# A linear-attention stage reordered: keys projected before the gate, and routing logits computed as 8 extra columns of the output product

## The reference

```
xxx = tanh((x + dx * maa_x) @ maa_w1);  mw, mk, mv, mr, mg = xxx_f @ maa_w2_f      # 5 factors
xf  = x + dx * (maa_f + m_f)                                                       # 5 inputs
r, k, v = xr @ W_r.T, xk @ W_k.T, xv @ W_v.T;  g = silu(xg @ W_g.T)
w = time_decay + tanh(xw @ decay_w1) @ decay_w2;  cs = cumsum(-exp(w))
A = lower ? (r*exp(cf)) (k*exp(-cf))^T : (r*exp(-cb)) (k*exp(cb))^T;  y = A @ v    # 16 heads of 8
y = groupnorm(y) * g @ W_o.T
x = layernorm(x + y)
logits = x @ gate_w.T;  probs = softmax(logits);  two best of 8 experts            # router of layer 2
```

## Time and profile before

| what | us |
|---|---|
| three timed runs | 1278.52, 1280.97, 1282.59 |
| median | 1280.97 |
| profiled execution, its own time | 1271.11 |
| its span | 1268.8 |
| the stage's first attention scores | 42.90 |
| the stage's last scatter instruction | ends near 392 |

### The profile page before, as it was taken

The page is one execution under the profiler, slowest core; times in us unless marked ns, Lnnn a source line. Parts: engine busy times, 40 slices in busy tenths (PEclk is TensorE's granted clock), DMA queues, the critical chain, the costliest instruction groups (busy, mean ns, idle before and its releaser), DMA issues. The chain is left out here.

```text
span 1268.8 us, 34315 instructions
## 1 busy us (share of the span) xinstructions
PE 963.4 (76%) x12701; PEld 681.3 (54%) x12702; DVE 799.1 (63%) x2290; ACT 576.5 (45%) x1143; POOL 490.6 (39%) x597
## 2 busy tenths in 40 slices
PE   6789999989852999972455463948899999614996
PEld 2456665666642999870222222737556665313885
DVE  3656777687553555542888885873587666852665
ACT  1454555555421555542555563323564443313664
POOL 0113434543472444444335330002034443443776
PEclk8787878889755999996667665975997675756998
DMA  2122212327011222213223123013211115001110
GB/s 88 34 60 68 77 37 59 85 69 221 21 45 54 62 58 57 60 33 97 43 51 74 42 34 104 26 67 98 69 55 53 52 52 176 11 15 51 54 53 23
DMA packets 121827, 78.88 MB, mean 62 GB/s; under 512 B 46947, under 2 KB 108361, under 8 KB 121312
## 3 DMA queue, kind: packets, MB, share of 16 engines
q1 hardware_dynamic: 115040, 64.36, 18.9%
q0 software_dynamic: 6656, 12.70, 3.2%
HBM read 48.46 MB, written 27.51 MB: 60 GB/s over the span
## 5 line engine op out<-in xcount | busy, mean ns | idle before, releaser
L1117 ACT ACTIVATE bx_h<-bx_up,bx_cur 128x128 f32<-128x128 f32 x288 | 82.3, 368 | 103.7 <-PE bx_up L1088 103.7
L571 POOL DMA_INDIRECT regions_b<-a_xo,a_seat x64 | 64.7, 1012 | 140.3 <-DVE a_seat L864 123.3
L686 ACT ACTIVATE a_at<-a_scores 128x1024 f32<-128x1024 f32 x64 | 65.6, 1025 | 99.6 <-PE a_scores L445 99.0
L1046 POOL DMA_INDIRECT chosen_b<-bx_ys,bx_to x72 | 75.5, 1048 | 91.1 <-DVE bx_ys L1160 91.1
L1088 PE MATMUL bx_up<-bx_xT,bx_cur 128*128 128x128 f32 x576 | 82.7, 287 | 0.7 <-DVE bx_cur L1133 0.2
L1070 PE MATMUL bx_down<-bk_w,bx_h 128*128 x576 | 82.0, 285 | 0.6 <-ACT bx_h L1117 0.4
L440 PE MATMUL a_scores<-a_rk,a_kx 32*128 32x128 f32 (+3 forms) x1024 | 64.9, 327 | 20.9 <-DVE a_kx L753 11.9
L1088 PEld LDWEIGHTS bx_up<-bx_xT,bx_cur 128*128 128x128 f32 x576 | 71.3, 195 | 10.5 <-issue 5.4
L1325 PE MATMUL c_bank<-c_sq,c_con 128*128 128x512 f32 x32 | 30.2, 1100 | 61.1 <-DVE keep_attn L1472 51.5
L598 POOL TENSOR_TENSOR a_vx<-a_vx,a_con 128x2048 f32<-128x2048 f32 x8 | 36.2, 4527 | 103.4 <-DMA a_vx<-lion_values 103.4
L440 PEld LDWEIGHTS a_scores<-a_rk,a_kx 32*128 32x128 f32 x1024 | 48.9, 218 | 43.8 <-issue 20.2
(11 more groups left out here) (426 smaller groups left out, 2633.9 us busy)
## 6 DMA issues: line engine op xcount, KB each, us to landing
a_vx<-lion_values SPq DMA_DIRECT2D x32, 256.0 KB
bx_xs<-regions_b SPq DMA_DIRECT2D x72, 65.0 KB, 1.8
bk_w<-in_b_w SPq DMA_DIRECT2D x16, 256.0 KB, 5.6
c_part<-chosen_b SPq DMA_DIRECT2D x16, 256.0 KB, 3.9
space<-in_d_w SPq DMA_DIRECT2D x16, 256.0 KB, 5.8
dx_xs<-regions_d SPq DMA_DIRECT2D x40, 65.0 KB, 1.8
a_xp<-in_a_xT SPq DMA_DIRECT2D x8, 256.0 KB, 4.2
a_xr<-in_x SPq DMA_DIRECT2D x8, 256.0 KB, 3.6
```

The costliest lines, as they stand in the source:

```text
L571: nc.gpsimd.indirect_dma_start(route["regions"], bass.IndirectOffsetOnAxis(ap=seat[b][:, k, t:t + 1], axis=0), xo[b][k][:, t, :], None).th ...
L686: op(at[m % 2][:], S4[:, :, 0:320].rearrange("p g (q k) -> p g q k", q=2)[:, :, :, 0:P], ACT.Copy).then_inc(s_ata, 1)
L1046: nc.gpsimd.indirect_dma_start(dest, bass.IndirectOffsetOnAxis(ap=to[u][:, 0:1], axis=0), ys[u][:], None, bounds_check=dest.shape[0] - 1, ...
L1117: i = op(h[u % 2][:, f, :], BU[u % 2][:, f * P:(f + 1) * P], act_fn, bias=cur[u % 2][:, FC * P + f:FC * P + f + 1])
```

## The change

It has five parts.

1. The output product gets a moving operand of 136 columns (`woe`: W_o and the 8 columns of W_o times the gate). Three tiles go to X2 at a pitch of 136 and the fourth goes, in slot 5, to the unused columns 320 to 455 of the last score bank. The four products of 8 columns are gone.
2. `sums` is split: `last_sum` reads the fourth tile ahead of slot 5's COPY_PREDICATED; the rest reads X2.
3. Keys and r are projected in slot 5 (banks X1 and X0) and the gate in slot 6 (bank X2). Keys are scaled at the end of VectorE's slot 5, r in slot 6, and the first half of the spread follows in slot 6. The gate's VectorE part goes to slot 7, ahead of `mix_input`. ScalarE's spread and gate swap places in the same way. A new semaphore `s_kk` says that the keys are scaled; the first scores now wait for `s_kd`, r scaled.
4. VectorE's second half of the spread moves from slot 1 to slot 3, ahead of the group norm.
5. One more load at the start: W_o into `woe`.

```diff
             def gate(k):
-                pe.wait_ge(s_ew, k + 1)
-                mm(X0, wT[:, 3, :], xf[4][:], start=True, stop=True).then_inc(s_g, 1)
+                if k >= 2:
+                    pe.wait_ge(s_z, k - 1)
+                mm(X2, wT[:, 3, :], xf[4][:], start=True, stop=True).then_inc(s_g, 1)
             def keys(k):
                 pe.wait_ge(s_vt, k + 1)
                 mm(X1, wT[:, 1, :], xf[1][:], start=True, stop=True)
-                if k >= 2:
-                    pe.wait_ge(s_z, k - 1)
-                mm(X2, wT[:, 0, :], xf[3][:], start=True, stop=True).then_inc(s_rk, 1)
+                pe.wait_ge(s_ew, k + 1)
+                mm(X0, wT[:, 0, :], xf[3][:], start=True, stop=True).then_inc(s_rk, 1)
             def turn_keys(k):
-                pe.wait_ge(s_gs, k + 1)
-                pe.wait_ge(s_kd, k + 1)
+                pe.wait_ge(s_kk, k + 1)
             def states(k):
                 pe.wait_ge(s_kt, k + 1)
+                pe.wait_ge(s_gs, k + 1)
             def project_out(n):
-                for t in range(GT):
-                    i = mm(X2[:, t * P:(t + 1) * P], yn[:, t * P:(t + 1) * P], wT[:, 4, :], start=True, stop=True)
+                for t in range(GT - 1):
+                    i = mm(X2[:, t * PE8:(t + 1) * PE8], yn[:, t * P:(t + 1) * P], woe[:], start=True, stop=True)
-            def yn_logits(out):
-                for t in range(GT):
-                    i = mm(out(t), yn[:, t * P:(t + 1) * P], wog[:], start=True, stop=True, skip_group_check=True)
-                return i
+            def project_last():
+                return mm(S4[:, GT - 1, 320:320 + PE8], yn[:, (GT - 1) * P:GTOK], woe[:], start=True, stop=True,
+                          skip_group_check=True)
 ...
+            def scale_r(k):
+                r = rk[k % 2]
+                v.tensor_tensor(r[:, 0, :], X0, ex[:, 1, 0, :], ALU.mult)
+                v.tensor_tensor(r[:, 2, :], X0, ex[:, 0, 1, :], ALU.mult).then_inc(s_kd, 1)
 ...
+            def last_sum(n):
+                v.tensor_tensor(z[:, last], S4[:, last, 320:320 + P], xr[n % 2][:, last], ALU.add)
+                then(v.tensor_tensor(rl[:, last], S4[:, last, 320 + P:320 + PE8], xg[n % 2][:, last], ALU.add))
 ...
                     elif m == 1:
-                        spread(n, 1)
                     elif m == 3:
+                        spread(n, 1)
                     elif m == 5:
                         if n:
                             sums(n - 1)
+                        if more:
+                            scale_keys(n + 1)
                     elif m == 6:
                         if more:
-                            gate(n + 1)
-                            scale_keys(n + 1)
+                            scale_r(n + 1)
+                            dve.wait_ge(s_kk, n + 2)
+                            spread(n + 1, 0)
                     elif m == 7:
                         if more:
-                            spread(n + 1, 0)
+                            gate(n + 1)
                             if n + 2 < NG:
                                 mix_input(n + 2)
```

More of the change, by code:

```diff
@@ L137, in lion_stage @@
     D_MIX, D_DECAY, NF = 32, 64, 5
+    PE8 = P + NE
     x_rows = x_in.rearrange("(g t p) c -> g p t c", t=GT, p=P)
@@ L206, in lion_stage @@
         won = sb("won", [P, P])
-        wog = sb("wog", [P, NE])
+        woe = sb("woe", [P, P + NE])
         gsum = sb("gsum", [P, NE])
@@ L333, in lion_stage @@
         NZ = 7 + 6 + 2
-        NW = 16 * (9 + NF)
+        NW = 16 * (10 + NF)
         @block.tensor
@@ L433, in scores @@
                 t, h, b = m // 2, m % 2, n % 2
+                if m == 0:
+                    pe.wait_ge(s_kd, n + 1)
                 if m % 4 == 0:
@@ L481, in step @@
                     if m == 5 and n:
-                        yn_logits(spare)
+                        project_last()
                     if m == 6 and more:
@@ L505, in step @@
                         elif m == 5:
+                            keys(n + 1)
+                        elif m == 6:
                             gate(n + 1)
-                        elif m == 6:
-                            keys(n + 1)
                         elif m == 7:
@@ L533, in _ @@
             decay_logits(0)
+            keys(0)
             gate(0)
-            keys(0)
             turn_keys(0)
@@ L541, in _ @@
             project_out(NG - 1)
-            yn_logits(lambda t: X0[:, t * NE:(t + 1) * NE]).then_inc(s_rl, 1)
+            project_last().then_inc(s_rl, 1)
             pe.wait_ge(s_pick, NG)
@@ L705, in step @@
                         elif m == 6:
+                            next_spread(n + 1)
+                        elif m == 7:
                             gate(n + 1)
-                        elif m == 7:
-                            next_spread(n + 1)
                             key_rows(n + 1)
@@ L727, in _ @@
             decay_factors(0)
+            next_spread(0)
             gate(0)
-            next_spread(0)
             key_rows(0)
@@ L793, in scale_keys @@
                 dve.wait_ge(s_rk, k + 1)
-                then(v.tensor_tensor(r[:, 1, :], X1, ex[:, 0, 0, :], ALU.mult))
-                v.tensor_tensor(r[:, 3, :], X1, ex[:, 1, 1, :], ALU.mult)
-                v.tensor_tensor(r[:, 0, :], X2, ex[:, 1, 0, :], ALU.mult)
-                v.tensor_tensor(r[:, 2, :], X2, ex[:, 0, 1, :], ALU.mult).then_inc(s_kd, 1)
+                v.tensor_tensor(r[:, 1, :], X1, ex[:, 0, 0, :], ALU.mult)
+                v.tensor_tensor(r[:, 3, :], X1, ex[:, 1, 1, :], ALU.mult).then_inc(s_kk, 1)
+            def scale_r(k):
+                r = rk[k % 2]
+                v.tensor_tensor(r[:, 0, :], X0, ex[:, 1, 0, :], ALU.mult)
+                v.tensor_tensor(r[:, 2, :], X0, ex[:, 0, 1, :], ALU.mult).then_inc(s_kd, 1)
             def state_mask(k):
@@ L808, in gated, with sums @@
                 v.scalar_tensor_tensor(yn[:], ya[:], lnwb[:, 1:2], gs[n % 2][:], ALU.add, ALU.mult).then_inc(s_yn, 1)
-            def sums(n):
+            def last_sum(n):
                 dve.wait_ge(s_xr[n % 2], 16 * (n // 2) + 16)
-                dve.wait_ge(s_o, n + 1)
                 if n:
                     dve.wait_ge(s_xb, n)
-                then(v.tensor_tensor(z[:], X2.rearrange("p (t c) -> p t c", t=GT), xr[n % 2][:], ALU.add))
+                last = GT - 1
+                v.tensor_tensor(z[:, last], S4[:, last, 320:320 + P], xr[n % 2][:, last], ALU.add)
+                then(v.tensor_tensor(rl[:, last], S4[:, last, 320 + P:320 + PE8], xg[n % 2][:, last], ALU.add))
+            def sums(n):
+                dve.wait_ge(s_o, n + 1)
+                out = X2[:, 0:(GT - 1) * PE8].rearrange("p (t c) -> p t c", t=GT - 1)
+                v.tensor_tensor(rl[:, 0:GT - 1], out[:, :, P:PE8], xg[n % 2][:, 0:GT - 1], ALU.add)
+                then(v.tensor_tensor(z[:, 0:GT - 1], out[:, :, 0:P], xr[n % 2][:, 0:GT - 1], ALU.add))
                 for t in range(GT):
@@ L877, in step @@
                     if m == 5 and n:
-                        then(v.tensor_tensor(rl[:], S4[:, :, 320:320 + NE], xg[1 - n % 2][:], ALU.add))
+                        last_sum(n - 1)
                     if m == 6 and more:
@@ L933, in _ @@
             running_sums(0)
+            scale_keys(0)
+            scale_r(0)
+            dve.wait_ge(s_kk, 1)
+            spread(0, 0)
             gate(0)
-            scale_keys(0)
-            dve.wait_ge(s_kd, 1)
-            spread(0, 0)
             mix_input(1)
@@ L942, in _ @@
             gated(NG - 1)
+            dve.wait_ge(s_rl, 1)
+            last_sum(NG - 1)
             sums(NG - 1)
-            dve.wait_ge(s_rl, 1)
-            then(v.tensor_tensor(rl[:], X0[:, 0:NE * GT].rearrange("p (t e) -> p t e", t=GT), xg[1][:], ALU.add))
             choose(NG - 1)
```

16 lines of the change are left out of this document (8 added, 8 removed).

## The result

The changed kernel takes 1271.8 us (median of 20 runs, 1265.65 to 1277.55), the kernel before on the same chips 1278.38 us (median of 20, 1270.36 to 1288.64). The ratio is 0.9959, 95% interval 0.994 to 0.9977: 6.6 us less by the medians, where 15 were forecast. The direction and the range were right; less than half of the size came.

A forecast was written before the change was run, and what follows sets the result against it. A step was taken as TensorE's work, waits for VectorE and the half-speed stretches behind them. Won boundaries -12, two earlier boundaries -1 each, last group and tail about -1: 1281 - 15 = 1266 us, own range 1258 to 1273, whole range 1250 to 1282.

The forecast's parts named there:

- won boundaries: Step boundaries where VectorE's spread escapes GpSimd's mask: part B -5.4 us, part A +1.9, so -3.5 each.
- the spread wins at three or four of five boundaries: At the five boundaries with scatter and mask, the spread mostly escapes the mask: -12 us in all.
- The lost boundary: Step boundary where the mask holds the spread: part B 16.1 to 17.5 us against 16.99, gain 0 (-0.9 to +0.5).
- lost race: Rival: the mask starts first at nearly every boundary, only -3 to -4 us remain, 1277 us; chance 0.30.
- Steps 0 and 1: The two earlier boundaries, without scatter: the step still ends with the mask, values come sooner, -1 us each.
- The last group and tail: End of the stage: fused logits at the low clock save about 1 us.
- seats, scatter, mask, spread: The chain said to set the boundary between steps; TensorE waited 1.17 us there, 3.31 in the last full step.
- the +1.9 for `mix_input` blocked by the mask: Start of a won step: the mask holds VectorE's `mix_input`, part A grows by 1.4 to 2.4 us, taken as 1.9.
- Slower: Rival: race lost, slot 7's copy late too, TensorE idles longer at the boundary, low clock lasts longer: 1287 us; chance 0.09.
- The move of the second spread: Part A, slot 1 to 3: removes a 0.70 us wait, seats don't move; 0, at best -1 us.
- Full gain: Rival: `mix_input` isn't held by the mask, a won step gives -6.9 us five times: 1244 us; chance 0.09.
- The logits: Fusing the branch's four 8-column products into the output product: net -0.82 us a step of TensorE, inside part B's chain.

The follow-up runs named there:

- eight products: The changed kernel with GpSimd's mask product written as eight of 256 columns, no wait added: 0.9882 of the kernel before.
- the logits alone: The kernel before, in its old order, with the routing logits as 8 more columns of the output product: 0.9972, then 0.9959 of the kernel before.

## Why the forecast was right in direction and wrong in size

Two steps failed: the count of won boundaries, and what a won one is worth.

**The first step that failed: "I take it that the spread wins at three or four of five boundaries".** It wins at none in the two profiles taken where before takes under 1280 us. Both runners were timed well. The spread starts 10.06 us after the seats (forecast 9.96), its fourth instruction could start about 10.8 after, and the mask starts 232.67 - 221.88 = 10.79 after, the lower end of 10.8 to 11.4. The error was to let the spread have "up to 0.6 us in hand and nothing against it but jitter". The values came earlier, so the wait of 0.59 us in front of the mask was gone, and all of the hand with it; the same sentence that gave the lower end should have decided. And the second instruction is lost, not the fourth: it begins 0.5 us after the last scatter has begun and ends only with that scatter, as the 0.54 us show where the mask comes later. With the mask right behind the scatter, it ends with the mask.

The Trainium skill (SBUF — State Buffer, "Who interferes with whom") says, as an inference, that descriptor generation needs the write interface of the shared pair; the 0.54 us that end with the scatter agree, while the instruction before, begun in the same scatter, took its plain 0.34 us and shows nothing of it. It says as well that whoever issues first keeps the pair. Against that stands the instruction that began 0.46 us before the first of eight products and was held for all of them (6.09 us): by this case's rows the measurement decides, and having come first was no protection behind a scatter.

**The lost boundary** was priced well: 16.1 to 17.5 us for part B, measured 238.26 - 221.88 = 16.38, -0.6 in the model step, of which part A gave 0.3 back. Over all five it came to -1.1 a step, a little past the end of its "0 (-0.9 to +0.5)", since before the boundaries themselves differed (a wait of 1.17 in the model step, 3.31 in the last). So the rival "lost race", -3 to -4 in all, had the mechanism, and half of the size. Steps 0 and 1 gave 1.4 where 2 stood. The last group and tail, put at -1, gave nothing: the last step was 1 to 3.6 us longer. The added load was put at 0. In the profiles with it the first values are stored at 28.7 to 29.1 us (four) or 31.0 to 31.1 (nine), in those without it at 28.1 to 28.7 (six) and 30.6 (one), so it may cost 0.5 us and more.

The direction came right without the mechanism that was to bring it: of the forecast -15, -12 were won boundaries, and none was won. This much is luck. What gave the 1.1 us a step instead is shown only in part: the wait at the boundary grew, one of two falls of the clock went, and the logits alone gave 0.3 to 0.4%.

One reading of before was wrong as well. The prediction let the boundary be set by "seats, scatter, mask, spread" and took the spread of the model step to end with the mask. That spread was held for 0.4 us (1.55 instead of 1.13); what the scores waited for was VectorE's own late work (with no mask on GpSimd they still wait 1.11 us), and only the last full step, with 3.70 us, was as described.

**The second step that failed: the won boundary was over-valued.** Its first term holds: -5.2 measured against -5.4 (part B 11.8 against 16.99). The second, the +1.9 for `mix_input` blocked by the mask, doesn't. The mechanism is as described, even to the 6.34 us at which the mixing products start, but part A became 215.24 - 189.20 = 26.04 us in the better half of the steps (+2.2), and 29.1 in the others (+5.3), by a fall of the clock that lasts 10.2 us instead of 3.4. Had all five been won, the time would have been the same within what is measured. This is the larger of the two errors: a term that is given back was sized from its wait, and the same wait of 3.54 us made part A longer by 2.2 us or by 5.3, by how long the clock stayed low behind it.

**"Slower"** had its mechanism too. The gap grew to 4.60 us and the fall of the clock behind it from 6.8 to 10.2 us. What it didn't foresee is that the other fall, at slots 2 and 3, went at the same time. The move of the second spread was given "0, at best -1" a step. **"Full gain"** is what comes when nothing holds VectorE: 1244 was worked out with `mix_input` free but the mask still in the way; without the mask the kernel takes 1221.

**The logits** were laid inside part B's chain and gave -0.3 and -0.4% alone, the first with an interval that reaches no change. That less work on TensorE counts wherever it runs at 1.2 GHz and nothing waits for VectorE would explain this; no run here isolates it.

## What to carry to other kernels

Where VectorE and GpSimd meet on long instructions, don't count who wins the race: count both sides, since the one that is moved out of the way stands in front of the next. Move the long GpSimd instruction to another engine (ScalarE had room here), or cut it in pieces and start it only when nothing of VectorE is under way, and look at what waits behind it on GpSimd. And price a wait of TensorE with the clock behind it: here steps with the same wait of 3.54 us took 37.9 or 40.9 us.

## What the runs showed of the hardware that was not expected

- A VectorE tensor-scalar instruction that began 0.5 us after the start of a GpSimd scatter of 0.96 us ended with the scatter (0.54 us instead of 0.34), and where a GpSimd product followed at once, it ended with that: 5.14 us with one of 4.51, 6.09 us with eight that take 5.5 together.
- Begun while the eight run, four such instructions take 3.10 us: each goes between two pieces.
- Where TensorE's longest gap was 0.90 us, the granted clock stayed at 1.00 for 218 us; with a gap of 3.5 us a step it fell once a step, for 3 to 10 us; behind a gap of 1.98 us it fell in four steps of five.
- The same kernel differs by group of runs: before took 1274 to 1275 us in three and 1302 to 1308 in three, and chip 13 had a group of each kind. In the profile of the changed kernel from a group of the second kind VectorE and TensorE stood idle beside the scatters, VectorE for up to 3.65 us. No run names the cause.
